# Splitting TensorE's two attention-times-V groups around the second pair of score matmuls, in a float32 transformer block on one core

## The chip, the cores and the metric

The kernel runs on one core of one Trainium2 chip. The metric is the device time of one execution in microseconds (us); 0.2% of it is 3.5 us. The profile adds one execution recorded instruction by instruction. The engines are PE (TensorE's matmuls), PEld (TensorE's weight loads), DVE (VectorE), ACT (ScalarE), POOL (GpSimd) and SP (SyncE, which issues DMAs).

## The reference

One transformer block with conditioning, for x of shape (4, 1024, 512), 16 heads of 32, in float32:

```
ada = silu(c) @ Wada.T + bada                      # shifts, scales and gates
h = modulate(rmsnorm(x, g1, D), scale_msa, shift_msa)
qkv = h @ Wqkv.T + bqkv
q = rmsnorm(q, gq, hd) * hd ** (-0.5);  k = rmsnorm(k, gk, hd)
attn = softmax(q @ k.T);  o = attn @ v
x = x + gate_msa * (o @ Wproj.T + bproj)
h = modulate(rmsnorm(x, g2, D), scale_mlp, shift_mlp)
x = x + gate_mlp * (gelu(h @ Wfc1.T + bfc1) @ Wfc2.T + bfc2)
```

## The kernel before, in words

Attention runs in 256 numbered steps L = 0 to 255, after 30 steps of start (L = -30 to -1); then comes the MLP. Each engine runs its own loop over L, written out by hand, and semaphores tie the loops together. A step covers four heads, 128 keys and 512 queries. Its parts:

- **Scores** `qk(L, p)`, p = 0 and 1 (line 558): two matmuls into the PSUM pair `scores[p]`. They wait until ACT has taken the exponentials of step L - 1 out of the same pair.
- **Exponentials** on ACT (line 784): two per step, into `probs[L % 3]`. The first of step L waits for `weigh(L - 3)` and for DVE's sum of step L - 3, since three `probs` buffers are there.
- **Weighing** `weigh(l)` (line 575): attention times V for step l, four matmuls with 32 columns of weights each, side by side in the array, into `pv`. A float32 matmul shows as two records, so one `weigh` is 8 records in the trace and 4 instructions in the program's order. All other matmuls named here use the full 128 x 128 array, apart from `row_sums` (lines 592 and 598), which also works in tiles of 32 columns. A run of such 32-column matmuls with nothing between them is called a **session** below.
- **Products** `fill(L, part)` (lines 645 and 658): the q, k and v projections of this and the next batch element. A table, `PLAN`, spreads each product of 12 matmuls over 1, 2 or 3 steps; half of a step's share is `part` 0 and half is `part` 1. All products accumulate in the one PSUM bank `gemm`, so the first matmul of a product waits until DVE has moved the last product out (`raw_out`, line 896, or `v_out`, line 906). FILL, the steps with products, ends at L = 207 (`PAIRED`). For L from 3 on there are 84 products: 53 start in an odd step and 31 in an even one. Until step 59 all of them start in odd steps.
- **Sums** on DVE (line 871): `probs` is added up, one addition of 128 x 2048 per step. In DVE's step L the order is: the last product's move-out, then `add(L - 1)`, then the pieces of the q and k norms.
- **Norm pieces**: `sum_squares` (lines 606, 610, 611), `turn` (transposes, line 622) on PE; logarithm, exponential and squares on ACT.

Through step 207, PE weighs in pairs: in each odd step, after all products of the step, it runs `weigh(L - 2)` and `weigh(L - 1)` as one session. From step 208 on it weighs once a step. `row_sums` (for L = 9, 17, 25, ..., always odd) stands between `qk(L, 0)` and `fill(L, 0)` up to L = `EARLY` = 80, and right ahead of the pair of weighings after that.

`TAIL` is 214. It places the loads and first splits of the MLP's inputs: POOL issues the loads of `heads_first` (line 1323) in its steps 216, 219, 222 and 225, and in step 216 it first waits for the last `part_lo`, which DVE makes in step 213. ACT splits them (line 1233) in steps 232 to 238.

Of the kernel before, what the change touches and what calls it, by code (L numbers as in the profile page):

```python
# [94 lines left out]
FILL = {step + i: (p, kind, b, g, x, i, steps) for p, (step, steps, b, kind, g, x) in enumerate(PLAN) for i in range(steps)}  # L95
# [9 lines left out]
def at_row(when):  # L105
    return {NT * (hh + 1) + when: hh for hh in range(NC * NG - 1)}


ROWS_AT, COMPACT_AT, INVERT_AT, INVERTED_AT, SPREAD_AT, OUT_AT = (at_row(x) for x in (ROWS, COMPACT, INVERT, INVERTED, SPREAD, OUT))
# [11 lines left out]
EARLY = 5 * STEPS  # L121
# [34 lines left out]
INV_AT, FIN_AT = ({step + after: n for step, n in SUM_AT.items()} for after in (1, 2))  # L156
LOW_AT = {step + (n >= HALVED): n for step, n in FIN_AT.items()}
# [4 lines left out]
def adds_until(l):  # L162

    hh, j = l // NT, l % NT
    return ADDS * min(hh, LEAN) + (ADDS - 1) * max(0, hh - LEAN) + (min(j, ADDS - 1) if hh >= LEAN else j)
# [6 lines left out]
    at = first + NT * (half + 1) + (-1 if kind == "k" else 3) if step >= 0 else step + 3  # L172
    STACK_LOAD.setdefault(max(step + 1, at), []).append(n)

TAIL = max(LOW_AT) + 1
PRODUCT_OF_UNIT = [p for p, x in enumerate(PLAN) if x[3] != "v"]
PRODUCT_OF_V = [p for p, x in enumerate(PLAN) if x[3] == "v"]
LOADED = 4
# [1 line left out]
PAIRED = max(FILL)  # L180
HEADS_LOAD, BIAS_LOAD, X_LOAD = {TAIL + 2 + 3 * t: t for t in range(CT)}, TAIL + 14, {TAIL + 17 + 3 * t: t for t in range(CT)}
HEADS_HIGH, HEADS_LOW, X_BIASED = ({TAIL + after + 2 * t: t for t in range(CT)} for after in (18, 19, 34))
MOD_LOAD, SCALE = 8, 14
# [171 lines left out]
def build_attention(nc, sem, small, dram, mem, psum, mlp):  # L355
# [181 lines left out]
    def tensor(pe):  # L537
# [3 lines left out]
        def qk(L, p):  # L541
            group, st = L // STEPS, L % STEPS
            half, j = st // NT, st % NT
            s = group % 2
            if p == 0:
                if st == 0 or st == NT // 2:
                    pe.wait_ge(k_in[s][st // (NT // 2)], 64 * (group // 2 + 1))
                if j == 0:
                    pe.wait_ge(q_in[half], 64 * (group + 1))
            if L > 0:  # L550

                pe.wait_ge(exp_done, 2 * (L - 1) + p + 1)
            elif p == 0:
                pe.wait_ge(h_moved, NT // 2)
                pe.wait_ge(h_moved_too, NT // 2)
            for i in range(2):
                h = 2 * p + i
                mm = nc.tensor.matmul(scores[p][:, i, :], k_stack[s][:, h, j * P:(j + 1) * P], q_stack[half][:, h, :],  # L558
                                      start=True, stop=True)
            mm.then_inc(qk_mm, 1)  # L560

        def weigh(l):
            b, g, j, hh = l // BSTEPS, l // STEPS % NG, l % NT, l // NT
            pe.wait_ge(exp_done, 2 * l + 2)
            if l == 0:

                last = max(p for p in range(FIRST_PRODUCTS) if p % 2 == 1)
                pe.wait_ge(v_moved if PLAN[last][3] == "v" else raw_done, NUMBER[last] + 1)
            if l % BSTEPS < NT:
                pe.wait_ge(v_moved, b * NT + j + 1)  # L570
            if j == 0 and hh >= NH:

                pe.wait_ge(o_done, hh - NH + 1)
            for h in range(HG):
                mm = nc.tensor.matmul(pv[hh % NH][h * DH:(h + 1) * DH, :], v[b % 2][:, j, (g * HG + h) * DH:(g * HG + h + 1) * DH],  # L575
                                      probs[l % RING][:, h, :], start=(j == 0), stop=(j == NT - 1))
            mm.then_inc(pv_mm, 1)

        def aux_free():

            if issued["squares"]:
                pe.wait_ge(ln_done, issued["squares"])
            if issued["turns"] > NT:
                pe.wait_ge(*moved(issued["turns"] - 1))
            if issued["rows"]:
                pe.wait_ge(rows_moved, issued["rows"])

        def row_sums(hh):
            pe.wait_ge(added, adds_until(NT * hh + NT - 1))
            aux_free()  # L590
            for h in range(HG):
                mm = nc.tensor.matmul(aux[h * DH:(h + 1) * DH, :], small["ones"][:], sums[:, h, :], start=True, stop=(hh < LEAN))  # L592
            if hh >= LEAN:

                l = NT * hh + NT - 1
                pe.wait_ge(exp_done, 2 * l + 2)
                for h in range(HG):
                    mm = nc.tensor.matmul(aux[h * DH:(h + 1) * DH, :], small["ones"][:], probs[l % RING][:, h, :], start=False, stop=True)
            mm.then_inc(rs_mm, 1)
            issued["rows"] += 1  # L600
# [33 lines left out]
        def unit_products(p, which, b, g, half, lo, hi):  # L634

            at = (0 if which == "q" else D) + g * P
            c = slice(half * CH, (half + 1) * CH)
            terms = [(w, h, k) for k in range(KT) for w, h in ((wq_hi, h_hi), (wq_hi, h_lo), (wq_lo, h_hi))]
            if lo == 0:
                bank_free(p)  # L640
                pe.wait_ge(lo_done, b * NT + (half + 1) * CT)
                pe.wait_ge(setup["low"], (1 if which == "k" else 2) + (3 if g > 0 else 0))
            for n in range(lo, hi):
                w, h, k = terms[n]
                mm = nc.tensor.matmul(bank_of_product(p)[:], w[:, k, at:at + P], h[:, k, c], start=(n == 0), stop=(n == len(terms) - 1))  # L645
            if hi == len(terms):
                mm.then_inc(unit_mm, 1)

        def v_products(p, b, t, lo, hi):
            c = slice(t * P, (t + 1) * P)  # L650
            terms = [(h, w, k) for k in range(KT) for h, w in ((h_hi, wq_hi), (h_hi, wq_lo), (h_lo, wq_hi))]
            if lo == 0:
                bank_free(p)
                pe.wait_ge(lo_done, max(CT, b * NT + t + 1))
                pe.wait_ge(setup["low"], 3)
            for n in range(lo, hi):
                h, w, k = terms[n]
                mm = nc.tensor.matmul(bank_of_product(p)[:], h[:, k, c], w[:, k, 2 * D:3 * D], start=(n == 0), stop=(n == len(terms) - 1))  # L658
            if hi == len(terms):
                mm.then_inc(v_mm, 1)  # L660

        def fill(L, part):
            if L not in FILL:
                return
            p, kind, b, g, x, i, steps = FILL[L]
            per = 3 * KT // steps
            lo = i * per + part * (per // 2)
            hi = lo + per // 2
            if kind == "v":
                v_products(p, b, x, lo, hi)  # L670
            else:
                unit_products(p, kind, b, g, x, lo, hi)

        setup["tensor_first"](pe)
        for L in range(START, AFTER):
            if L >= 0:
                qk(L, 0)
            if L in ROWS_AT and L <= EARLY:
                row_sums(ROWS_AT[L])
            fill(L, 0)  # L680
            if L >= 0:
                qk(L, 1)
            if L in ROWS_AT and L > PAIRED:
                row_sums(ROWS_AT[L])
            fill(L, 1)
            if L in SUM_AT:
                sum_squares(SUM_AT[L])
            if L in ROW_MM:
                setup["tensor_row"](pe, ROW_MM[L])
            if L in TURN_AT:  # L690
                turn(TURN_AT[L])
            if L == MOD_TURN:
                setup["tensor_turn"](pe)
            if L == NT:
                pe.wait_ge(ada_made, NA_LATER)
            if L in ROWS_AT and EARLY < L <= PAIRED:
                row_sums(ROWS_AT[L])
            if L > PAIRED:
                weigh(L - 1)
            elif L > 0 and L % 2 == 1:  # L700

                if L > 1:
                    weigh(L - 2)
                weigh(L - 1)
            if L == ADA_MM:
                for k in range(KT):
                    for i, r in enumerate(ada_rows):
                        if k == 0:
                            pe.wait_ge(ada_w_in[i], 16)
                        mm = nc.tensor.matmul(pv[1][r, :], silu[:, k, :], ada_w[i][:, k, :], start=(k == 0), stop=(k == KT - 1))  # L710
                mm.then_inc(ada_mm, 1)
# [143 lines left out]
    def vector(dve):  # L855
# [172 lines left out]
        mlp_last(lambda: invert(last), lambda: output(last))  # L1028

    return dict(sync=sync, tensor=tensor, scalar=scalar, gpsimd=gpsimd, vector=vector)  # L1030


# [821 lines left out]
```

## Time and profile before

| what | value |
|---|---|
| device time, three runs | median 1774.96 us (1774.0 to 1777.69) |
| the profiled execution | 1777.33 us |
| its span, first to last instruction | 1775.5 us |
| PE busy | 1716.7 us, 97% |
| PEld busy | 1151.9 us, 65% |
| DVE busy | 1054.5 us, 59% |
| ACT busy | 976.0 us, 55% |

The profiled execution lasts 1.8 us longer than its span and stands 2.4 us above the median. Busy is the time in which at least one instruction of the engine runs. Matmuls overlap: one of 512 columns is recorded as about 390 ns long while the next starts 230 ns after it, so a busy PE may still lose time between matmuls. What a place costs on PE is read from the distance between the starts of matmuls.

Attention's steps 0 to 59 lie from 63 to 317 us of the span, steps 60 to 207 from 317 to 830 us, steps 208 to 255 from 830 to 956 us, and the MLP after that.

### The profile page before, as it was taken

To read this page: it belongs to the slowest core of one execution; us is meant where nothing else is said; L and a number is where in the kernel's file an instruction comes from. 1 tells how busy PE (TensorE), PEld (TensorE's weight loads), DVE (VectorE), ACT (ScalarE), POOL (GpSimd) and SP (SyncE) were. 2 spreads that over 40 slices of the span, in tenths; PEclk is the share of its full clock that TensorE was granted. 3 is DMA by queue.
4 is the path that set the end of the run, shared out by engine and by line. 5 is a ranking of instruction groups with operands and counts; after the bars stand their busy time and mean duration, and the time that the engine had idled before them with its cause. 6 is when DMAs were issued, how large, how long until landed. Compare 5 with 4: busy or idle time off the path is not lost.

```text
span 1775.5 us, 23481 instructions
## 1 busy us (share of the span) xinstructions
PE 1716.7 (97%) x8436; PEld 1151.9 (65%) x8436; DVE 1054.5 (59%) x1269; ACT 976.0 (55%) x1272; POOL 393.9 (22%) x303
## 2 busy tenths in 40 slices
PE   7999999999999999999999999999999999999999
PEld 4555554555555555554334787888888888888887
DVE  5678887889998899888687444141332324141311
ACT  4577777798888888879897432222222222222221
POOL 2001110111111111000150233333332333333332
PEclk9999999999999999999999899999999999999999
DMA  7555554555565554655775202010020202010000
GB/s 279 139 137 144 131 142 127 132 138 149 138 162 131 138 147 129 158 141 145 175 159 209 65 18 61 23 54 24 14 69 6 65 18 65 18 53 24 14 22 24
DMA packets 122244, 176.94 MB, mean 100 GB/s; under 512 B 29568, under 2 KB 43904, under 8 KB 121136
## 3 DMA queue, kind: packets, MB, share of 16 engines
q1 hardware_dynamic: 119648, 163.75, 34.5%
q10 hardware_dynamic: 1712, 9.47, 1.4%
q0 software_dynamic: 800, 2.62, 0.6%
q8 instruction: 50, 0.82, 0.2%
q14 instruction: 34, 0.28, 0.1%
HBM read 124.87 MB, written 50.92 MB: 99 GB/s over the span
## 4 chain that ended last, share of the span: by engine, by line
PE 74%; DVE 12%; ACT 7%; issue 4%; DMA 2%; SPq 1%; POOL 0%; ACTq 0%; DVEq 0%
PE scores L1446 19%; PE pv L1463 10%; PE gemm L1463 10%; PE scores L558 8%; PE pv L575 7%; DVE sums L871 7%; PE gemm L645 6%; ACT probs L784 5%; PE pv L1418 4%; PE gemm L658 4%; PE aux L592 2%; DVE raw L896 1%; DMA parts_scratch<-parts 1%; DVE h_full L936 1%; PE aux L1433 1%
## 5 line engine op out<-in xcount | busy, mean ns | idle before, releaser
L784 ACT ACTIVATE probs<-scores,shift 128x1024 f32<-128x1024 f32 x512 | 549.9, 1115 | 141.9 <-PE scores L558 133.3
L871 DVE TENSOR_TENSOR sums<-sums,probs 128x2048 f32<-128x2048 f32 x186 | 440.0, 2366 | 26.4 <-ACT probs L784 23.6
L558 PE MATMUL scores<-q_stack,k_stack 128*128 128x512 f32 x1024 | 349.2, 425 | 5.5 <-ACT probs L784 4.3
L1446 PE MATMUL scores<-w_hi,act_parts 128*128 128x512 f32 x1016 | 315.0, 391 | 0.0
L558 PEld LDWEIGHTS scores<-q_stack,k_stack 128*128 128x128 f32 x1024 | 172.2, 188 | 191.8 <-issue 92.0
L1378 POOL TENSOR_TENSOR act_parts<-act_full,act_parts 128x512 fp32r<-128x512 f32 x127 | 170.4, 1342 | 477.2 <-ACT act_parts L1309 477.2
L575 PE MATMUL pv<-probs,v 128*32 128x512 f32 x2048 | 251.3, 599 | 2.3 <-DVE o_out L881 1.9
L1446 PEld LDWEIGHTS scores<-w_hi,act_parts 128*128 128x128 f32 x1016 | 189.2, 188 | 38.3
L1309 ACT ACTIVATE act_parts<-act_full 128x512 fp32r<-128x512 f32 x127 | 80.3, 632 | 219.7 <-PE scores L1446 218.8
L1446 PE MATMUL scores<-w_lo,act_parts 128*128 128x512 f32 x508 | 197.9, 389 | 0.0
L1522 DVE TENSOR_TENSOR y_next<-pv,p_bias 128x512 f32<-128x512 f32 x28 | 19.3, 691 | 298.5 <-PE pv L1418 298.5
L1463 PE MATMUL gemm<-z,w 128*128 128x512 f32 x768 | 187.1, 393 | 2.6 <-DVE z L1627 2.6
L1463 PE MATMUL pv<-z,w 128*128 128x512 f32 x768 | 185.7, 391 | 0.0
L1463 PEld LDWEIGHTS gemm<-z,w 128*128 128x128 f32 x768 | 145.7, 190 | 33.4 <-DVE z L1627 3.0
L1463 PEld LDWEIGHTS pv<-z,w 128*128 128x128 f32 x768 | 144.0, 188 | 29.9
L1295 ACT ACTIVATE act_full<-gemm,f_bias 128x512 f32<-128x512 f32 x64 | 44.2, 690 | 186.7 <-PE gemm L1463 181.4
L575 PEld LDWEIGHTS pv<-probs,v 128*32 128x32 f32 x2048 | 53.1, 109 | 124.6 <-issue 109.8
L645 PE MATMUL gemm<-h_hi,wq_hi 128*128 128x512 f32 x248 | 103.9, 419 | 22.4 <-DVE raw L896 12.0
L1295 ACT ACTIVATE act_full<-pv,f_bias 128x512 f32<-128x512 f32 x64 | 44.0, 688 | 147.4 <-PE pv L1463 146.0
L840 POOL TENSOR_TENSOR h_lo<-h_full,h_hi 128x512 fp32r<-128x512 f32 x26 | 73.2, 2817 | 217.0 <-ACT h_hi L765 217.0
L1446 PEld LDWEIGHTS scores<-w_lo,act_parts 128*128 128x128 f32 x508 | 95.4, 188 | 20.1
L845 POOL TENSOR_TENSOR x_inv<-x_sqc,minus_half 128x1 f32<-128x1 f32 x32 | 18.8, 589 | 390.5 <-DVE x_sqc L918 390.5
(195 smaller groups left out, 2059.6 us busy)
## 6 DMA issues: line engine op xcount, KB each, us to landing
k_stack<-parts_scratch SPq DMA_DIRECT2D x128, 256.0 KB, 5.0
q_stack<-parts_scratch SPq DMA_DIRECT2D x128, 256.0 KB, 5.1
parts_scratch<-parts SPq DMA_DIRECT2D x62, 512.0 KB, 3.1
inverse<-inverse_scratch SPq DMA_DIRECT2D x128, 64.0 KB, 2.0
heads_out<-o_out SPq DMA_DIRECT2D x32, 256.0 KB, 4.7
out<-result SPq DMA_DIRECT2D x30, 256.0 KB, 2.0
heads<-heads_out SPq DMA_DIRECT2D x28, 256.0 KB, 3.9
x_tile<-in_x SPq DMA_DIRECT2D x28, 256.0 KB, 2.8
```

Of the source, the lines that this page charges most:

```text
L558: mm = nc.tensor.matmul(scores[p][:, i, :], k_stack[s][:, h, j * P:(j + 1) * P], q_stack[half][:, h, :], start=True, stop=True)
L575: mm = nc.tensor.matmul(pv[hh % NH][h * DH:(h + 1) * DH, :], v[b % 2][:, j, (g * HG + h) * DH:(g * HG + h + 1) * DH], probs[l % RING][:, h ...
L645: mm = nc.tensor.matmul(bank_of_product(p)[:], w[:, k, at:at + P], h[:, k, c], start=(n == 0), stop=(n == len(terms) - 1))
L658: mm = nc.tensor.matmul(bank_of_product(p)[:], h[:, k, c], w[:, k, 2 * D:3 * D], start=(n == 0), stop=(n == len(terms) - 1))
L784: nc.scalar.activation(probs[L % RING][:, 2 * p:2 * p + 2, :], scores[p][:], ACT.Exp, bias=small["shift"][:]).then_inc(exp_done, 1)
L840: nc.gpsimd.tensor_tensor(h_lo[:, :, c], buffer_of_turn(n)[:], full(h_hi[:, :, c]), ALU.subtract).then_inc(lo_done, 1)
L871: nc.vector.tensor_tensor(sums[:], a[:], probs[l % RING][:], ALU.add).then_inc(added, 1)
L1295: nc.scalar.activation(act_full[m % 2][:], up[m % 2], ACT.Gelu_apprx_tanh, bias=f1_bias[:, m:m + 1]).then_inc(gelu_done, 1)
L1309: nc.scalar.activation(parts_of(c, m)[:, 0, :], act_full[m % 2][:], ACT.Copy).then_inc(act_hi, 1)
L1378: nc.gpsimd.tensor_tensor(parts_of(c, m)[:, 1, :], act_full[m % 2][:], full(parts_of(c, m)[:, 0, :]), ALU.subtract).then_inc(act_lo, 1)
L1446: mm = nc.tensor.matmul(acc[t], parts_of(c, m)[:, b, t * P:(t + 1) * P], w2[a][:, m, :], start=(m == 0 and i == 0), stop=(m == NM - 1 and ...
L1463: mm = nc.tensor.matmul(up[m % 2], w1[a][:, m, k, :], z[b][:, k, :], start=(k == 0 and i == 0), stop=(k == KT - 1 and i == 2))
```

## The change

In every odd step L > 1 that has products, PE's order becomes: `qk(L, 0)`, `weigh(L - 2)`, `qk(L, 1)`, `weigh(L - 1)`, both halves of the products, then the norm pieces. `row_sums` keeps its place up to L = 80; after that it stands behind `qk(L, 1)`, ahead of `weigh(L - 1)`. Even steps and all steps from 208 on are as before. `TAIL` becomes 212, the last entry of FIN_AT.

```
-TAIL = max(LOW_AT) + 1
+TAIL = max(FIN_AT)
...
         for L in range(START, AFTER):
+            weigh_first = L > 1 and L % 2 == 1 and L in FILL
             if L >= 0:
                 qk(L, 0)
             if L in ROWS_AT and L <= EARLY:
                 row_sums(ROWS_AT[L])
-            fill(L, 0)
+            if weigh_first:
+                weigh(L - 2)
+            else:
+                fill(L, 0)
             if L >= 0:
                 qk(L, 1)
-            if L in ROWS_AT and L > PAIRED:
+            if L in ROWS_AT and (L > PAIRED or weigh_first and L > EARLY):
                 row_sums(ROWS_AT[L])
+            if weigh_first:
+                weigh(L - 1)
+                fill(L, 0)
             fill(L, 1)
...
-            if L in ROWS_AT and EARLY < L <= PAIRED:
+            if L in ROWS_AT and EARLY < L <= PAIRED and not weigh_first:
                 row_sums(ROWS_AT[L])
             if L > PAIRED:
                 weigh(L - 1)
-            elif L > 0 and L % 2 == 1:
+            elif L > 0 and L % 2 == 1 and not weigh_first:
```

This is PE's order in step 57, where a v product starts (`gemm` is its bank, `pv<-probs` is a weighing, `aux<-sums` is `row_sums`). First before, from `qk(57, 0)` to the first scores of step 58:

```order
L558 MATMUL scores<-q_stack_69,k_stack_67 128x512 x2
L592 MATMUL aux<-sums,ones 32x512 x4
L658 MATMUL gemm<-wq_hi,h_hi 128x512
L658 MATMUL gemm<-wq_lo,h_hi 128x512
L658 MATMUL gemm<-wq_hi,h_lo 128x512
L558 MATMUL scores<-q_stack_69,k_stack_67 128x512 x2
L658 MATMUL gemm<-wq_hi,h_hi 128x512
L658 MATMUL gemm<-wq_lo,h_hi 128x512
L658 MATMUL gemm<-wq_hi,h_lo 128x512
L575 MATMUL pv<-probs_73,v_70 32x512 x4
L575 MATMUL pv<-probs_74,v_70 32x512 x4
L558 MATMUL scores<-q_stack_69,k_stack_67 128x512 x2
```

And after the change:

```order
L558 MATMUL scores<-q_stack_69,k_stack_67 128x512 x2
L592 MATMUL aux<-sums,ones 32x512 x4
L575 MATMUL pv<-probs_73,v_70 32x512 x4
L558 MATMUL scores<-q_stack_69,k_stack_67 128x512 x2
L575 MATMUL pv<-probs_74,v_70 32x512 x4
L658 MATMUL gemm<-wq_hi,h_hi 128x512
L658 MATMUL gemm<-wq_lo,h_hi 128x512
L658 MATMUL gemm<-wq_hi,h_lo 128x512
L658 MATMUL gemm<-wq_hi,h_hi 128x512
L658 MATMUL gemm<-wq_lo,h_hi 128x512
L658 MATMUL gemm<-wq_hi,h_lo 128x512
L558 MATMUL scores<-q_stack_69,k_stack_67 128x512 x2
```

The product's first matmul moved behind both weighings and the second pair of scores. The count of sessions is two in both.

The second place is the border of steps 157 and 158 on PE: a q product ends in step 157 and a v product starts in step 158. Before, from `qk(157, 1)` on:

```order
L558 MATMUL scores<-q_stack_69,k_stack_67 128x512 x2
L645 MATMUL gemm<-h_lo,wq_hi 128x512
L645 MATMUL gemm<-h_hi,wq_lo 128x512
L610 MATMUL aux<-squares_hi,head_ones 128x512
L611 MATMUL aux<-squares_lo,head_ones 128x512
L575 MATMUL pv<-probs_74,v_70 32x512 x4
L575 MATMUL pv<-probs_72,v_70 32x512 x4
L558 MATMUL scores<-q_stack_69,k_stack_67 128x512 x2
L658 MATMUL gemm<-wq_hi,h_hi 128x512
```

And after the change, from `qk(157, 0)` on:

```order
L558 MATMUL scores<-q_stack_69,k_stack_67 128x512 x2
L575 MATMUL pv<-probs_74,v_70 32x512 x4
L558 MATMUL scores<-q_stack_69,k_stack_67 128x512 x2
L575 MATMUL pv<-probs_72,v_70 32x512 x4
L645 MATMUL gemm<-h_hi,wq_lo 128x512
L645 MATMUL gemm<-h_hi,wq_hi 128x512
L645 MATMUL gemm<-h_lo,wq_hi 128x512
L645 MATMUL gemm<-h_hi,wq_lo 128x512
L610 MATMUL aux<-squares_hi,head_ones 128x512
L611 MATMUL aux<-squares_lo,head_ones 128x512
L558 MATMUL scores<-q_stack_69,k_stack_67 128x512 x2
L658 MATMUL gemm<-wq_hi,h_hi 128x512
```

Between the end of one product and the start of the next, the two weighings are gone, and one session became two.

## Rows read from the trace of the kernel before

**Rows 1.** The page, part 1: busy time, share, instructions

```profile
PE 1716.7 (97%) x8436; PEld 1151.9 (65%) x8436; DVE 1054.5 (59%) x1269; ACT 976.0 (55%) x1272; POOL 393.9 (22%) x303
```

**Rows 2.** Busy us (x instructions) by stretch, then clock, DMA share, GB/s

```profile
core 0: us, PE busy (x) PEld busy (x) DVE busy (x) ACT busy (x) POOL busy (x), PEclk, DMA share, GB/s
63.00:317.00 254.00, 239.40 (x1220) 138.23 (x1224) 202.97 (x224) 185.24 (x225) 23.42 (x19) 0.99 0.51 136
317.00:830.00 513.00, 499.15 (x2726) 277.87 (x2719) 448.98 (x421) 439.76 (x546) 60.46 (x29) 1.00 0.55 141
```

**Rows 3.** Timeline, end of step 171: start us, length us, engine, line, tiles

```profile
706.86 0.40 PE L645 MATMUL gemm<-h_hi,wq_hi 128*128 128x512 f32 x1
...
707.18 1.92 PE L575 MATMUL pv<-probs,v 128*32 128x512 f32 x16
...
709.04 0.73 PE L558 MATMUL scores<-q_stack,k_stack 128*128 128x512 f32 x2
...
709.61 0.39 PE L645 MATMUL gemm<-h_lo,wq_hi 128*128 128x512 f32 x1
```

**Rows 4.** Timeline, step 210, where a session holds one weighing

```profile
838.61 0.40 PE L611 MATMUL aux<-squares_lo,head_ones 128*128 128x512 f32 x1
...
838.93 1.06 PE L575 MATMUL pv<-probs,v 128*32 128x512 f32 x8
...
839.93 1.54 PE L558 MATMUL scores<-q_stack,k_stack 128*128 128x512 f32 x4
```

**Rows 5.** Timeline of PE, step 25: row sums, then a product

```profile
172.16 1.07 PE L592 MATMUL aux<-sums,ones 128*32 128x512 f32 x8 [0.35 <-issue]
173.15 0.50 PE L645 MATMUL gemm<-h_hi,wq_hi 128*128 128x512 f32 x1
```

**Rows 6.** Waits of PEld, 63 to 317 us: total, times, longest

```profile
PEld gemm L645 <- DVE raw L896: 15.6, 13, 3.0
PEld gemm L645 <- DVE v L906: 4.3, 5, 1.6
...
PEld gemm L658 <- DVE raw L896: 3.6, 4, 1.8
...
PEld gemm L658 <- DVE v L906: 2.4, 3, 0.8
```

**Rows 7.** Waits of PEld, 317 to 830 us

```profile
PEld scores L558 <- ACT probs L784: 28.9, 67, 0.8
PEld gemm L658 <- DVE raw L896: 13.7, 15, 2.2
...
PEld gemm L645 <- DVE raw L896: 9.3, 14, 1.5
PEld gemm L645 <- DVE v L906: 6.2, 13, 0.8
```

**Rows 8.** Timeline, steps 170 and 171: a product ends, the next starts

```profile
703.67 0.62 PE L558 MATMUL scores<-q_stack,k_stack 128*128 128x512 f32 x2
...
704.13 0.40 PE L645 MATMUL gemm<-h_lo,wq_hi 128*128 128x512 f32 x1
...
704.36 0.39 PE L645 MATMUL gemm<-h_hi,wq_lo 128*128 128x512 f32 x1
...
704.79 0.75 DVE L896 TENSOR_SCALAR raw<-gemm,qk_bias 128x512 f32<-128x512 f32 x1 [0.26 <-PE gemm L645]
...
705.60 0.19 PEld L645 LDWEIGHTS gemm<-h_hi,wq_hi 128*128 128x128 f32 x1 [0.38 <-DVE raw L896]
```

**Rows 9.** Timeline, step 158: a product starts in an even step

```profile
661.07 0.73 PE L558 MATMUL scores<-q_stack,k_stack 128*128 128x512 f32 x2
661.25 0.74 DVE L896 TENSOR_SCALAR raw<-gemm,qk_bias 128x512 f32<-128x512 f32 x1
...
662.04 0.19 PEld L658 LDWEIGHTS gemm<-wq_hi,h_hi 128*128 128x128 f32 x1 [0.68 <-DVE raw L896]
662.04 0.50 PE L658 MATMUL gemm<-wq_hi,h_hi 128*128 128x512 f32 x1 [0.24 <-DVE raw L896]
662.15 0.19 PEld L658 LDWEIGHTS gemm<-wq_lo,h_hi 128*128 128x128 f32 x1
662.38 0.40 PE L658 MATMUL gemm<-wq_lo,h_hi 128*128 128x512 f32 x1
```

**Rows 10.** Waits of ACT, 317 to 830 us

```profile
ACT probs L784 <- PE scores L558: 64.4, 78, 1.9
```

**Rows 11.** Timeline of POOL: the first load of the MLP's heads

```profile
852.70 0.95 POOL L1323 DMA_DIRECT2D y<-heads_out  x1 [139.06 <-issue]
```

## The prediction

> **What bounds the kernel now.** The change sits in steps 3 to 207, so I looked at that stretch only. The page comes first [rows 1]: PE is busy for 97% of the span, with DVE and ACT far behind. By stretch the picture is closer [rows 2]: from 317 to 830 us PE is busy 499 of 513 us (97%), DVE 449 (88%) and ACT 440 (86%); from 63 to 317 us they are at 94%, 80% and 73%. So PE is first, and the other two follow closely in the later stretch.
>
> Busy time hides what PE loses, so I read starts. In an undisturbed stream full-array matmuls start 0.23 us apart: the two score matmuls at 703.67 take 0.46 us until the next product matmul, and that one 0.23 until the next [rows 8]. Two things break the stream. One is a session of 32-column matmuls. The other is the start of a product, whose first weight load waits for DVE to move the last product out [rows 6, 7]. The sum is made of these two.
>
> The Trainium skill ("Perfetto Trace Analysis", Identifying the Most-Contended Engine) says that matmul busy time is a bad measure and that the busy share of weight loads is a good one. By the weight loads [rows 2] TensorE works 278 of 513 us, 54%, which would leave DVE as the most contended engine and would make extra time on PE free. The starts speak against it here: nearly all of PE's time is taken by matmuls at their closest spacing or by a session. I take the starts, and keep the page's reading as a rival, worked out from rows below.
>
> **Term A: more sessions.** A session of two weighings spreads the last full matmul ahead of it and the first behind it 709.04 - 706.86 = 2.18 us apart [rows 3]. With one weighing it is 839.93 - 838.61 = 1.32 us [rows 4]. So a weighing costs 0.86, and a session by itself 1.32 - 0.86 = 0.46 where an undisturbed distance is 0.23: 0.23 lost. The two score matmuls behind a session then take 709.61 - 709.04 = 0.57 until the next start [rows 3], not 0.46 [rows 8]: 0.11 more. A session more costs 0.34 us. The change also puts a product behind a session; the nearest row is a product behind row sums, whose first matmul starts 0.99 after the session's start [rows 5], as scores do in step 210 (1.00) [rows 4], so the price is the same.
>
> How many more: odd steps 3 to 207 are 103. Where row sums stand at L up to 80 (9 to 73, nine steps) there were two sessions and there are two; in later steps with row sums they already shared the session of the weighings and still share one. So 103 - 9 = 94 more, 94 x 0.34 = **+32 us**. It lies on the path wherever PE doesn't wait anyway. "TensorEngine Tiling (Array Packing)", Key Properties, of the Trainium skill says that changing the tiling mode drains TensorE. It names no price; it speaks against this change, and without such a drain A would be nothing and the sum below lower by 32.
>
> **Term B: product starts in odd steps.** The first product matmul now comes behind two sessions and four score matmuls, about 2.5 us later (the wait for DVE counts from the end of the last product, and that end, in an even step, isn't moved). What is lost at such a start is PEld's idle time less 0.17: in step 158 the idle is 0.68 [rows 9], while the product starts 0.97 after the scores where 0.57 is undisturbed [rows 3], and its second matmul 0.34 after the first and not 0.23, together 0.51. Until 317 us the waits sum to 25.9 us in 25 starts, less 25 x 0.17 gives 21.6 [rows 6]. All but steps 0 and 2 start in odd steps. Step 1 isn't changed (0.6), and the longest (3.0) keeps a few tenths: 20 go. From 317 us on it is 29.2 in 42 starts, less 42 x 0.17 gives 22 [rows 7]. Of these, even starts have about 9: seven like step 158 at 0.51, two long ones (the longest row, 2.2) at 2.0, the rest 0.1 each. The odd ones' 13 go. B = **-33 us**. Bounds: all of the 43.6 read as odd and gone, -43; or, if DVE is late by more than the 2.5 us in some, -28.
>
> **Term C: product starts in even steps.** Here the change takes cover away. Before, a product that ended in an odd step had the session of two weighings behind it: DVE could start up to 2.5 us late and the next product still lost only 0.1 to 0.5. Now only two score matmuls stand between. The smallest distance from a product's last matmul to the next product's first, with DVE free, is 705.60 - 704.36 = 1.24 us [rows 8]; the undisturbed one is 3 x 0.23 = 0.69. That loses 0.55, and 0.11 for the second matmul: 0.65 per start. Of the 31 even starts, 12 have a `sum_squares` ahead of them at the end of the odd step (as step 158), which gives 0.46 of cover: 0.1 to 0.3 each. 19 have none: 19 x 0.65 = 12.4. With 12 x 0.25 = 3 and 3.5 for the two long ones, where DVE is late by more than that, even starts lose 19 in place of 9. C = **+10 us**. Bounds: +4 (the later end of the product finds the stall of the two long ones and of the seven gone, and DVE always free) to +25 (DVE late by half an addition more at each).
>
> **Term D: waits for exponentials.** `qk(L, 1)` of an odd step now stands behind `weigh(L - 2)`, 0.6 us later, and no longer catches ACT at work. PEld's idle time for scores, released by ACT, is 28.9 us in 67 [rows 7], but most of it is the ordinary wait behind a session that ends with ACT's signal as the last one. I take -2, between 0 and -5. `qk(L, 0)` waits as before, since the even step ahead of it is the same.
>
> **Term E: TAIL.** POOL's loads wait for a signal of DVE's step 213 in either kernel, and POOL has nothing else queued: the first goes out at 852.70 after 139 us of nothing [rows 11]. Moving it from POOL's step 216 to 214 moves no issue in time. ACT's four splits come two steps earlier, the same number in the same stage. 0, between -1 and +1. What covers it is the rest of attention, to 956 us; if that were gone, a load moved by two steps would cost what it is late, at most its few us once.
>
> **Sum.** 32 - 33 + 10 - 2 = +7 us on the profiled execution's 1777.33: 1784. That execution stood 2.4 above the median 1774.96, so against the median it is **1782 us**.
>
> **Rivals.**
> - *DVE becomes the bound (slower by more).* In DVE's program the addition of step L stands behind the move-out in step L + 1, and that now waits until the end of the odd step. DVE is at 88% [rows 2]. If each of the 31 even starts holds an addition up by 0.5 us and it isn't made good, C grows by 15: 1797. For it: the high share. Against: the pair gets longer by 0.34, which gives DVE room. From 2 or 3 tenths of DVE's time per pair on it decides. Chance 0.15.
> - *TensorE isn't the bound (the other side).* ACT waits for scores 64.4 us in 78 times from 317 to 830 us [rows 10], all while PE is in its double session. With the scores of p = 1 between the two weighings, ACT gets them spread out, DVE's additions come earlier, and its lateness at starts of both kinds goes. Then sessions are paid from time in which PE waited: B -40, C +2, D -5, with A 32: -11, so 1764. It needs DVE on time at three quarters of the starts. For it: ACT's long waits. Against: a free DVE still loses 0.65 per even start, and ACT isn't what PE waits for most. Chance 0.25 for anything faster than -3.5, the likeliest of it near 1768. The page's reading of TensorE ends here as well, since it would make A free.
> - *The terms cancel (no change).* A and C at the low end, B at the middle: 30 - 33 + 6 - 2 = +1, 1776. Chance 0.2.
> - *The forecast,* +3.5 to +15: chance 0.4.
>
> **How the numbers follow.** Faster 0.25; within 0.2% (3.5 us, about what a measurement of this kernel can tell from no change) 0.2; slower 0.4 + 0.15 = 0.55. The range leaves out the far tenth on each side: from 1767, most of the way into the fast rival, to 1796, up to the DVE rival. The forecast's own range is 1778 to 1790.
>
> **What the changed kernel's profile would show.** A: in odd steps two rows of 8 weighing records with a score pair between, each pair behind one with 0.73 length; PE's record count as before. B: the stretch up to step 59 shorter than 254 us by about 12 (20 saved, 22 sessions x 0.34 = 7.5 paid), with waits of `gemm` for DVE nearly gone there. C: after that the stretch to step 207 longer than 513 us by about 19, waits of `gemm` loads at even starts at 0.7 to 1 us each. E: first head load still right behind the last `part_lo`. The prediction is wrong if the second stretch doesn't grow: then either sessions overlap with waits or DVE was late for a reason that the new order removes. It is wrong the other way if DVE's additions wait for move-outs and ACT for additions.

## The result: 1800 us, slower by 1.35%

| | before | after |
|---|---|---|
| device time, four runs each | 1776.33 us (1774.0 to 1779.04) | 1800.28 us (1798.96 to 1801.02) |
| ratio | | 1.0135 (95% interval 1.0123 to 1.0147) |
| span of the profiled execution | 1775.5 us | 1797.1 us |
| steps 0 to 59 | 255.4 us | 258.7 us |
| steps 60 to 207 | 512.7 us | 532.8 us |
| steps 208 to 255 | 123.7 us | 122.5 us |

A stretch of steps goes here from the first score matmul of its first step to the first one behind its last step; the last row ends at the first score matmul of step 255, since none comes behind it. In the kernel before, step 60 starts at 318.3 us and step 208 at 831.0, 1.3 and 1.0 us later than the 317 and 830 that the forecast went by; this moves none of its terms. The kernel is slower by 24 us where +7 was forecast. The later stretch grew by 20.1 us (forecast 19.5). The early one, which was to shrink by 12, grew by 3.3. The miss is there.

The page of the kernel after, part 1 (as [rows 1]) and part 4, the chain that ended last, by engine:

```profile
PE 1740.0 (97%) x8436; PEld 1138.0 (63%) x8436; DVE 1054.4 (59%) x1269; ACT 977.7 (54%) x1272; POOL 385.4 (21%) x303
PE 82%; DVE 10%; ACT 5%; issue 2%; DMA 1%; SPq 0%; POOL 0%; DVEq 0%; ACTq 0%
```

PE's busy time rose by 23 us and its share stayed, because the profile counts as busy what is lost between matmuls. The number of PE instructions is the same (8436). Busy time by stretch, before and then after; the columns are those of [rows 2], the stretches those of the table:

```profile
62.90:318.30 255.40, 240.77 (x1229) 138.49 (x1229) 204.27 (x225) 186.07 (x227) 23.88 (x20) 0.99 0.52 136
318.30:831.00 512.70, 498.85 (x2722) 277.84 (x2718) 448.79 (x421) 439.99 (x545) 60.00 (x29) 1.00 0.55 140
```

```profile
61.70:320.40 258.70, 244.13 (x1229) 134.59 (x1230) 205.97 (x226) 183.37 (x225) 19.95 (x19) 0.99 0.51 135
320.40:853.20 532.80, 518.92 (x2720) 268.23 (x2719) 448.00 (x422) 444.90 (x546) 55.87 (x29) 1.00 0.53 135
853.20:975.70 122.50, 117.17 (x656) 38.94 (x654) 92.67 (x54) 107.78 (x112) 28.81 (x19) 1.00 0.62 150
```

DVE and ACT work nearly as long as before in each stretch (in the later one DVE 449 and then 448 us, ACT 440 and 445), and the granted clock is the same. So the time is in the order, not in slower instructions. To find it I went through the starts of PE's matmuls and took from each distance the undisturbed one of [rows 3, 4, 8]; what is left is a stall, named by what stands ahead of it and behind it. A sum of many stalls depends on the undisturbed distance that is taken off, and is good to about 1 us:

| us of stall on PE | before | after | forecast |
|---|---|---|---|
| **steps 1 to 59**, sessions | 37 | 59 | +22, +7.5 us |
| product starts, both their matmuls | 19.0 | 4.5 | -20 |
| row sums, waiting for the sum | 1.4 | 9.2 | 0 |
| sum of squares at the end of an even step | 0 | 1.7 | 0 |
| all stalls of the stretch | 30.0 | 26.9 | -20 |
| **steps 60 to 206**, sessions | 75 | 146 | +72, +24.5 us |
| product starts in odd steps, both matmuls | 13.2 | 0.3 | -13 |
| product starts in even steps, both matmuls | 9.3 | 15.5 | +10 |
| scores of odd steps behind products, waiting for ACT | 1.7 | 6.4 | 0 |
| second matmul of the score pairs in odd steps | 5.6 | 3.6 | -2 |
| all stalls of the stretch | 32.7 | 29.1 | -5 |

The later part of the table ends where step 207 starts, so it has 71 new sessions and not 72. Sessions at 0.34 us and stalls add up to the change over the same steps: 22 x 0.34 - 3.1 = +4.4 us (measured +3.3), and 71 x 0.34 - 3.6 = +20.5 us (measured +19.7).

**Where the early 20 us went.** PE's waits from 61.7 to 320.4 us, which answer to [rows 6], total, times, longest:

```profile
PEld aux L592 <- DVE sums L878: 6.5, 3, 2.4
...
PEld gemm L645 <- DVE raw L903: 5.1, 4, 1.9
...
PEld gemm L645 <- DVE v L913: 3.4, 3, 1.7
...
PEld gemm L658 <- DVE raw L903: 2.9, 2, 2.0
...
PEld gemm L658 <- DVE v L913: 1.6, 2, 0.8
```

The waits at product starts did shrink, from 25.9 us in 25 starts to 13.0 in 11, and of those 13.0 0.84 each is the ordinary pause of a load behind a session (a row with it, 674.87, is shown below), so 3.8 us are lost, near the 4.5 of the table. The first row is new: `row_sums` (L592) waits for DVE's addition. It stands in PE's queue ahead of `weigh(L - 2)`, which has no reason to wait. DVE's own waits in the same stretch show why its addition is late:

```profile
DVE sums L878 <- ACT probs L791: 18.5, 11, 4.2
DVE h_full L943 <- PE aux L622: 8.5, 4, 2.6
```

Before, `h_full` waited 0.5 us in 2 times. `h_full` moves the four transposes of `turn` out of PSUM, and in DVE's order the next addition stands behind it. In the new order `turn` comes last in PE's step. Step 35 and the start of step 36 in the timeline, first before, then after (DVE and PE rows):

```profile
213.63 2.28 DVE L871 TENSOR_TENSOR sums<-sums,probs 128x2048 f32<-128x2048 f32 x1
...
215.47 0.60 PE L622 MATMUL aux<-ident,xt 128*128 128x128 f32 x4
...
216.11 1.37 DVE L936 TENSOR_SCALAR h_full<-aux,scale,mod 128x128 f32<-128x128 f32 x4 [0.20 <-PE aux L622]
...
217.40 2.28 DVE L871 TENSOR_TENSOR sums<-sums,probs 128x2048 f32<-128x2048 f32 x1
```

```profile
212.97 2.28 DVE L878 TENSOR_TENSOR sums<-sums,probs 128x2048 f32<-128x2048 f32 x1
...
217.22 0.60 PE L622 MATMUL aux<-ident,xt 128*128 128x128 f32 x4
...
217.85 1.36 DVE L943 TENSOR_SCALAR h_full<-aux,scale,mod 128x128 f32<-128x128 f32 x4 [2.60 <-PE aux L622]
219.14 2.28 DVE L878 TENSOR_TENSOR sums<-sums,probs 128x2048 f32<-128x2048 f32 x1
```

The addition ahead of it ends 0.66 us earlier than before, the next one starts 1.74 us later. The 2.4 us between the two are the wait in brackets, 2.60 where it was 0.20: DVE stands still, because both sessions of the step, which came behind `turn`, now stand ahead of it. In step 41, after one more such `turn` in step 39, PE waits 1.94 us for an addition at the row sums (new kernel):

```profile
236.41 2.28 DVE L878 TENSOR_TENSOR sums<-sums,probs 128x2048 f32<-128x2048 f32 x1
...
238.74 1.06 PE L592 MATMUL aux<-sums,ones 128*32 128x512 f32 x8 [1.94 <-DVE sums L878]
```

**Where the later 20 us come from.** A session's end and an even start of the new kernel, steps 157 and 158, which answer to [rows 9]:

```profile
674.87 0.19 PEld L645 LDWEIGHTS gemm<-h_hi,wq_lo 128*128 128x128 f32 x1 [0.84 <-issue]
...
675.67 0.40 PE L645 MATMUL gemm<-h_hi,wq_lo 128*128 128x512 f32 x1
...
676.11 0.75 DVE L903 TENSOR_SCALAR raw<-gemm,qk_bias 128x512 f32<-128x512 f32 x1
...
676.38 0.62 PE L558 MATMUL scores<-q_stack,k_stack 128*128 128x512 f32 x2
...
676.91 0.50 PE L658 MATMUL gemm<-wq_hi,h_hi 128*128 128x512 f32 x1
```

The product in step 158 starts 676.91 - 676.38 = 0.53 us behind the scores, so it loses 0.07 us, where it took 0.97 before. The even starts that have no `sum_squares` ahead of them now lose time instead, and all even starts sum to 15.5 us. The later stretch is thus made of term A's 24 us and of stalls that nearly cancel.

### The profile page after: what moved, and what is told of

Read it like the earlier page. It is cut to its first block, busy times and chain, and to the rows that moved or that the text cites. A ratio compares the mean times of both kernels' runs of the same rounds, so it can differ in the third digit from the quotient of the medians.

```text
span 1797.1 us, 23481 instructions
## 1 busy us (share of the span) xinstructions
PE 1740.0 (97%) x8436; PEld 1138.0 (63%) x8436; DVE 1054.4 (59%) x1269; ACT 977.7 (54%) x1272; POOL 385.4 (21%) x303
## 4 chain that ended last, share of the span: by engine, by line
PE 82%; DVE 10%; ACT 5%; issue 2%; DMA 1%; SPq 0%; POOL 0%; DVEq 0%; ACTq 0%
PE scores L1453 19%; PE pv L575 10%; PE scores L558 10%; PE pv L1470 10%; PE gemm L1470 10%; PE gemm L645 8%; DVE sums L878 5%; PE gemm L658 4%; PE pv L1425 4%; ACT probs L791 3%; PE aux L592 2%; PE aux L606 1%; PE aux L1440 1%; DVE h_full L943 1%; DVE v L913 1%
## 5 line engine op out<-in xcount | busy, mean ns | idle before, releaser
L878 DVE TENSOR_TENSOR sums<-sums,probs 128x2048 f32<-128x2048 f32 x186 | 437.5, 2352 | 25.1 <-ACT probs L791 21.9
L558 PE MATMUL scores<-q_stack,k_stack 128*128 128x512 f32 x1024 | 348.1, 424 | 10.2 <-ACT probs L791 9.2
L575 PE MATMUL pv<-probs,v 128*32 128x512 f32 x2048 | 273.2, 605 | 0.5 <-ACT probs L791 0.4
L847 POOL TENSOR_TENSOR h_lo<-h_full,h_hi 128x512 fp32r<-128x512 f32 x26 | 65.3, 2510 | 226.9 <-ACT h_hi L772 226.9
L575 PEld LDWEIGHTS pv<-probs,v 128*32 128x32 f32 x2048 | 43.6, 108 | 102.0 <-issue 73.1
```

What stands on the lines that cost most here:

```text
L878: nc.vector.tensor_tensor(sums[:], a[:], probs[l % RING][:], ALU.add).then_inc(added, 1)
```

## The experiments

Each kernel is the kernel before with one edit to PE's order, and each was timed in five rounds against the kernel before on the same chip. `TAIL` is as before in all but the tenth. The condition `weigh_first` of the change says in which odd steps the new order holds.

**1 and 2. Early steps alone, later steps alone.**

```
-            weigh_first = L > 1 and L % 2 == 1 and L in FILL
+            weigh_first = 1 < L < 60 and L % 2 == 1                  # first kernel
+            weigh_first = L >= 60 and L % 2 == 1 and L in FILL       # second kernel
```

> The new order in odd steps 3 to 59 alone; TAIL and all steps from 60 on as before. In the changed kernel steps 0 to 60 took 258.7 us (61.7 to 320.4) against 255.4 before, where I had forecast 12 less. If that miss is a thing of this stretch by itself (theory: DVE becomes late there and stays late), this kernel reads 3 to 5 us above before, and steps 0 to 60 last 258 to 260 us. Rival: the early gain is there, and is lost because the later steps' order reaches back through buffers; then this kernel is 8 to 12 us faster than before.

Measured: 1780.04 against 1775.99 us, ratio 1.0024 (1.0014 to 1.0035): +4.0 us.

> The new order in odd steps 61 to 207 alone. Terms A, C and the later part of B are what acts here: 72 sessions x 0.34 = +24.5, odd starts -13, even starts +10, waits for exponentials -2: +19.5 us over before, 1796. In the changed kernel steps 60 to 208 took 532.8 us against 512.7, which is +20. Rival: the loss needs the lateness that DVE brings along from the early steps; then +10 or less.

Measured: 1794.16 against 1775.99 us, ratio 1.0102 (1.0086 to 1.0117): +18.2 us. The two add to +22.2 us of the +24. The later part is as forecast; the early one costs time where it was to save 12.

**3. Transposes ahead of the products.** The first kernel, with `turn` right behind `weigh(L - 1)` in its odd steps:

```
             if weigh_first:
                 weigh(L - 1)
+                if L in TURN_AT:
+                    turn(TURN_AT[L])
                 fill(L, 0)
...
-            if L in TURN_AT:
+            if L in TURN_AT and not weigh_first:
                 turn(TURN_AT[L])
```

> As s1_only, and in odd steps with a turn (four transposes) those stand ahead of the step's products, behind weigh(L - 1), so that they end about 1.4 us sooner. Theory: the early gain is lost since DVE's h_out, which is queued ahead of add(L), waits for transposes that now come last in the odd step (8.5 us of such waits in the changed kernel against 0.5 before, in four places). Then those waits fall to 2 to 4 us, DVE is late by less at row sums and at the next starts, and the time is 4 to 8 us below s1_only. Rival (row sums are what waits, whatever DVE does; or DVE is simply full): within 2 us of s1_only.

Measured: 1775.08 against 1775.99 us, ratio 0.9997 (0.9988 to 1.0006), which is 5.0 us less than the first kernel. DVE's and PE's waits of it, 62.6 to 316.1 us:

```profile
DVE h_full L945 <- PE aux L622: 2.7, 4, 1.2
```

```profile
PEld aux L622 <- DVE xt L932: 5.5, 4, 2.5
...
PEld aux L592 <- DVE sums L880: 3.9, 3, 1.9
```

DVE's wait fell from 8.5 to 2.7 us. The row of L622 is the price: at its new place `turn` is early for its own input in four steps. The late transposes are a cause, but not the only reason why the row sums wait: their row is still 3.9 us, where it is 6.5 in the first kernel (shown in experiment 4). What else makes those additions late for PE was not separated.

**4. Row sums behind `qk(L, 1)`.** The first kernel, with early row sums where the change has the late ones:

```
-            if L in ROWS_AT and L <= EARLY:
+            if L in ROWS_AT and L <= EARLY and not weigh_first:
                 row_sums(ROWS_AT[L])
...
-            if L in ROWS_AT and (L > PAIRED or weigh_first and L > EARLY):
+            if L in ROWS_AT and (L > PAIRED or weigh_first):
```

> As s1_only, with the row sums of these steps behind qk(L, 1) and ahead of weigh(L - 1), where the later ones are. Rival theory: what was gained at starts is lost because row_sums stands right behind qk(L, 0) and waits for DVE's addition (9 us in seven steps in the changed kernel, 1.4 before) while weigh(L - 2) could run; then the time is 6 to 9 us below s1_only. Theory (DVE itself is late through the transposes): the wait only moves on to the product's start or the next additions, and the time is 0 to 3 us below s1_only.

Measured: 1772.75 against 1775.99 us, ratio 0.9984 (0.9975 to 0.9993), 7.3 us less than the first kernel. PE's waits in the first kernel, 62.5 to 321.2 us:

```profile
PEld aux L592 <- DVE sums L878: 6.5, 3, 2.5
...
PEld gemm L645 <- DVE raw L903: 6.0, 5, 1.9
```

DVE's and PE's waits in this one, 62.5 to 314 us:

```profile
DVE h_full L943 <- PE aux L622: 8.8, 4, 2.6
```

```profile
PEld aux L592 <- DVE sums L878: 1.9, 3, 0.8
...
PEld gemm L645 <- DVE raw L903: 8.8, 6, 2.4
```

My theory, that the place of the row sums is a symptom worth 0 to 3 us, fell, and the rival was right. `h_full` waits as long as in the full change, so DVE is no earlier; but the weighing ahead of the row sums now fills part of the time. A part moved on to the product starts (6.0 to 8.8 us). The number of sessions is 59 in both kernels, since the row sums only change from the session of `weigh(L - 2)` to that of `weigh(L - 1)`, so all of the 7.3 us are waits.

**5. Both at once.** Edits 3 and 4 in one kernel.

> s1_turn_first and s1_rows_later together, steps 3 to 59 alone. Alone they gave -5.0 and -7.3 us against s1_only. If late transposes and early row sums are two causes side by side, -10 to -12: 1768 to 1770. If they are one (either takes away the same lateness of DVE), -7 to -8: 1772 to 1773. My forecast of the stretch had been -12.5 against before, which would be 1763.5.

Measured: 1769.56 against 1775.99 us, ratio 0.9964 (0.9951 to 0.9978), 10.5 us less than the first kernel. 5.0 + 7.3 = 12.3: two causes side by side with an overlap of 2. Its steps 0 to 59 take 247.5 us where the kernel before takes 255.4 and the change 258.7. So these two edits get 8 of the forecast 12 us. In its trace product starts still lose 3.8 us and `turn` loses 2.1 waiting for its own input.

**6. One session of two weighings.** The change, with both weighings ahead of `qk(L, 1)`, and from step 81 on the row sums between them:

```
             if weigh_first:
                 weigh(L - 2)
+                if L in ROWS_AT and L > EARLY:
+                    row_sums(ROWS_AT[L])
+                weigh(L - 1)
             else:
                 fill(L, 0)
...
             if weigh_first:
-                weigh(L - 1)
                 fill(L, 0)
```

> The changed kernel's order, but both weighings in one session ahead of qk(L, 1) in all odd steps 3 to 207: qk(L, 0), weigh(L - 2), weigh(L - 1), qk(L, 1), products (row sums after step 80 between the weighings; TAIL as before). It leaves the late products, the late transposes and the short cover of even starts as they are and takes 103 sessions away. Term A says 103 x 0.34 = 35 us less than the changed kernel: 1765, 11 below before. Rival (TensorE's sessions are paid from waiting time, and what costs is the products' place): 1795 or more.

Measured: 1792.74 against 1775.99 us, ratio 1.0094 (1.0079 to 1.0109): only 7.5 us less than the full change. Neither theory holds as written. The sessions went (103 fewer, -35 us by term A), but stalls grew: from 26.9 to 30.2 us in steps 1 to 59, and from 29.1 to 50.9 in steps 60 to 206, of them 19.1 in place of 6.4 at the scores of odd steps behind products. ACT's and PE's waits in the later stretch, first of the change (320 to 853 us), then of this kernel (315 to 847 us), which also answer to [rows 7, 10]:

```profile
ACT probs L791 <- PE scores L558: 53.3, 83, 1.8
```

```profile
PEld scores L558 <- ACT probs L791: 42.2, 58, 2.0
```

```profile
ACT probs L793 <- PE scores L558: 81.9, 98, 2.6
```

```profile
PEld scores L558 <- ACT probs L793: 52.4, 65, 2.0
...
PEld aux L592 <- DVE sums L880: 10.9, 13, 1.5
```

With the double session ahead of `qk(L, 1)` ACT waits for its scores 82 us in place of 53, so it is later with the exponentials, and PE waits for those; its row sums wait for the additions, which are late with them. The second session costs 0.34 us and hands ACT its second pair one weighing sooner. Most of what it costs comes back there: 7.5 us of 35 are left.

**7 to 9. Later steps by their kind.** The 74 later odd steps are 24 in which a product starts, 32 in which one ends and 18 in its middle. Steps 73 (an end) and 65 (a middle) have early row sums and so two sessions in either order, which leaves 31 and 17 new sessions; the expectations counted one step too few for the ends and one too many for the middles. The new order in one kind each:

```
+            weigh_first = L >= 60 and L % 2 == 1 and L in FILL and FILL[L][5] == 0                    # starts
+            weigh_first = L >= 60 and L % 2 == 1 and L in FILL and FILL[L][5] == FILL[L][6] - 1       # ends
+            weigh_first = L >= 60 and L % 2 == 1 and L in FILL and 0 < FILL[L][5] < FILL[L][6] - 1    # middles
```

> The new order from step 60 on only in the 24 odd steps in which a product starts. Even starts keep their double session as cover, so term C falls away: 24 x 0.34 = +8, odd starts -13, exponentials -1: -6 us against before, 1770. s2_only had +18.2. Rival (what costs from step 60 on is the sessions and what they do to ACT and DVE, not the even starts): +18.2 x 24 / 72 = +6, 1782.

Measured: 1772.78 against 1775.99 us, ratio 0.9983 (0.9974 to 0.9992): -3.2 us, about half of the -6 expected. In its trace the 13.2 us at odd product starts are gone, but the scores of odd steps behind products lose the same 6.4 us for ACT as in the whole change. In the kernels of experiments 8 and 9 they stay under 2 us, so term D's miss comes from the start steps.

> The new order from step 60 on only in the 19 odd steps in which a product neither starts nor ends. Nothing of terms B and C is in it; 18 sessions more (step 65 has early row sums) at 0.34 = +6 us, 1782, if a session is paid in full. Rival (a session between the two score pairs feeds ACT more evenly and is half paid by waits that it takes away, which one_session's small gain hints at): +3 or less.

Measured: 1780.49 against 1776.29 us, ratio 1.0022 (1.0012 to 1.0031): +4.2 us, between the two: 0.25 us for each of the 17 new sessions. At 0.34 us these sessions would cost 5.8 us. In its trace stalls shrink by some 2.5 us from step 60 on, 1.7 of it at odd product starts (13.2 to 11.5), whose steps weren't changed. What is left, 3.3 us, is near the 3 us by which steps 60 to 207 grew (512.7 to 515.8): a session costs no less here, but stalls elsewhere pay a part of it.

> The new order from step 60 on only in the 31 odd steps in which a product ends, so that the next starts in the even step behind. 30 sessions more = +10 us and term C = +10: 1796. Against s2_only (+18.2), s2_starts (-3.2) and s2_mid (+6) additivity asks for +15 to +16. Rival (C is nothing, since DVE was late at those starts anyway): +10, 1786.

Measured: 1800.37 against 1776.29 us, ratio 1.0133 (1.0113 to 1.0154): +24.1 us, as slow as the whole change, with a third of its new sessions. PE's waits from 318 to 856 us:

```profile
PEld gemm L645 <- DVE raw L903: 16.2, 21, 1.9
...
PEld gemm L658 <- DVE raw L903: 15.3, 16, 3.3
...
PEld gemm L645 <- DVE v L913: 12.1, 16, 0.8
```

Its sessions went from 75 to 105 (+10.2 us) and its stalls from 32.7 to 47.6 us (+14.9); together +25.1, and steps 60 to 207 last 537.9 us, 25.2 more. Stalls at even starts rose from 9.3 to 17.3 us, and those at product starts in odd steps from 13.2 to about 19, though nothing was moved in those: DVE is late there too. Alone the three kinds sum to -3.2 + 4.2 + 24.1 = +25.1, together they are +18.2. So the new order in start steps is worth 18.2 - 24.1 - 4.2 = -10 us once the end steps have it, and -3 without: the stall that it takes away at odd starts is about 19 us in the one case and 13.2 in the other.

**10. TAIL alone.**

```
-TAIL = max(LOW_AT) + 1
+TAIL = max(FIN_AT)
```

> TAIL = 212 alone, nothing else changed: 0, within 1.5 us of before, since POOL's loads wait for DVE's step 213 in either. Rival: ACT's four splits meet other work in steps 230 to 236, +-2 us.

Measured: 1776.53 against 1776.29 us, ratio 0.9999 (0.9989 to 1.0008): nothing.

**11. New order where a product starts, one session.** In odd steps with `FILL[L][5] == 0` (29 early, 24 later) both weighings and row sums between them stand ahead of `qk(L, 1)`, and `turn` ahead of the products; all else is as before. From step 60 on every `turn` lies in an even step, so that part acts in the early steps alone.

> All that the theory asks for: only in the 53 odd steps in which a product starts, with both weighings in one session ahead of qk(L, 1), row sums between them, transposes ahead of the products. No session more than before (in 7 steps with early row sums one less, -2), even starts keep their cover, odd starts lose their stalls. Early stretch -20 at most, of which 12 to 18 if DVE keeps up, later -13 and -2: 1776 - 30 = 1746, between 1742 and 1756. Rival (DVE and ACT are so full that they take over): not below 1765.

Measured: 1767.3 against 1775.99 us, ratio 0.9952 (0.9938 to 0.9966): -8.7 us. Steps 0 to 59 take 245.0 us, 10.4 less than before, and steps 60 to 207 take 512.8, as long as before. The -30 us expected were far off, and the rival held. Later, odd starts lose nothing any more, but the scores of odd steps behind products lose some 19 us waiting for ACT, as in experiment 6. Early, 245.0 us is 2.5 less than with the split sessions of experiment 5; experiment 12 has the same early order and takes 246.7, so the lead of one session is 1 to 2.5 us, where 29 sessions less would have given 10.

**12. The parts that pay.** As 11 through step 59; from 60 on the split order in start steps.

```
+            weigh_first = L > 1 and L % 2 == 1 and L in FILL and FILL[L][5] == 0
+            together = weigh_first and L < 60
```

> In the 53 odd steps in which a product starts: up to step 59 both weighings in one session ahead of qk(L, 1), with the row sums between them (in best1 steps 1 to 60 lasted 241.2 us, 10.4 less than before); from step 60 on the changed kernel's split order (s2_starts: steps 60 to 207 at 505.2, in best1 508.4); transposes ahead of the products. -10.4 and -3.2: 1762 to 1764. Rival (the two stretches don't add up): 1767, as best1.

Measured: 1763.12 us (1762.28 to 1767.1) against 1776.29, ratio 0.993 (0.9914 to 0.9946): -13.2 us, faster than both kernels. Its stretches, with the columns of [rows 2]:

```profile
62.40:309.10 246.70, 235.02 (x1229) 138.12 (x1230) 204.93 (x225) 181.83 (x225) 18.96 (x19) 1.00 0.53 140
309.10:819.10 510.00, 501.19 (x2719) 275.31 (x2717) 449.30 (x421) 441.58 (x547) 54.87 (x29) 1.00 0.55 142
```

8.7 us come from the first stretch, 2.7 from the second and 2.1 from steps 208 to 255 (123.7 to 121.6), where nothing was changed. That last stretch lies between 121.4 and 124.7 us in the traces of all fourteen kernels (before, after and twelve experiments), which have the same order on PE there, so the 2.1 us can't be put down to this edit.

## Why the prediction was right in direction and wrong in size

The direction was right, the size (+24 us for +7) wasn't, and 1800.28 lies above the range.

- **Term B, early: the step that failed.** "20 go" of the 21.6 us until 317 us. By the distances between starts there were 19.0 us, and 14.5 of them went (19.0 to 4.5), but 8 came back at the row sums and 2 at the sum of squares of even steps, 2 more came in small pieces elsewhere, and all stalls together fell by 3. B took DVE's move-out as the only wait, and as one that is counted from the product's end alone. It left out that what was moved ahead of the products pushes everything behind them in PE's step: `turn` came 2.4 us later against DVE's addition (step 35), and DVE waits for it with an addition queued behind. Experiments 3 to 5 show both halves, 5.0 and 7.3 us, 10.5 together, and with them the early stretch comes to 247.5 us; the forecast was about 243. Of the 7.8 us at the row sums the transposes explain only a part (experiment 3); what else makes those additions late stays open. This is the rival "DVE becomes the bound" in kind, with its condition (additions that wait) met in the early stretch and through another instruction than the one I named.
- **Term A** was right in count and in price where the change is read as a whole: sessions at 0.34 us and the stalls account for both stretches within 1.1 us. Experiment 8 has a net of 0.25 us for a session, since stalls elsewhere shrink. What was wrong is that A stands by itself: experiment 6 takes the sessions away and gets 7.5 us of 35 back, because the split also brings ACT's scores forward. The rival "TensorE isn't the bound" said that sessions would be paid from PE's waits. That is true in part, but it needed DVE on time, and DVE was later.
- **Term B, later:** -13 forecast, -12.9 measured. **Term C:** +10 forecast, +6.2 in the change. Done alone, the end steps cost far more (experiment 9), which C couldn't see: it priced even starts with DVE free, and DVE isn't.
- **Term D** had the wrong sign: -2 forecast. The second matmuls of odd steps' score pairs lose 2.0 less, but the first pair behind a product loses 4.7 more, of which I wrote that it "waits as before, since the even step ahead of it is the same". The step is the same; what stands ahead of it isn't, and ACT comes into it later. Experiment 7 puts it on the start steps. C and D erred by 4 and 5 us against each other, and the later stretch came out within 0.6 us partly for that reason.
- **Term E:** 0, measured 0.2 in experiment 10.
- **The trace's busy shares.** I had set the Trainium skill's reading ("Perfetto Trace Analysis", Identifying the Most-Contended Engine: judge TensorE by its weight loads) against the starts of matmuls. In steps 60 to 207 the loads' share fell from 277.84/512.70 = 54% to 268.23/532.80 = 50% while the time grew by 20 us. By its direction the trace agrees with it, since the same work took longer. By its level the trace doesn't: 54% would leave room for new sessions, and 71 of them at 0.34 us were paid with only 3.6 us of stalls to set against them. On a change of tiling mode the Trainium skill ("TensorEngine Tiling (Array Packing)", Key Properties) says that it drains TensorE. The trace agrees in so far as each session costs time at its ends, 0.34 us; that this time is a drain, no row shows.

Two things stay open: why steps 208 to 255 differ by up to 3 us between kernels that don't differ there, and what besides the transposes makes the additions late at the row sums.

## What to carry to other kernels

Where something is moved ahead in an in-order queue, list what it pushes back, and for each of those the engine that waits and what that engine has queued behind the wait: here four small transposes, up to 2.4 us later, held up an addition, and putting them first gave 5.0 of the 15 us back by which the early stretch missed its forecast. Move work ahead only in the steps where it hides a wait (13 us faster), not in all of them (24 us slower). And a cost that is read between two matmuls of one engine isn't all to be had by taking it away, when its place also sets when the next engine can start.

## What the hardware showed that I had not expected

- A session of 32-column matmuls between full-array ones costs 0.34 us at its ends, read from the starts. But 103 more of them, in a kernel whose PE is at 97%, made 7.5 us (1800.28 against 1792.74) and not 35, because the same split hands ACT its scores sooner.
- DVE at 88% busy in a stretch is already late at the places that count. Its busy time there stayed within 1 us (448.8 before, 448.0 after, 449.7 in experiment 9), while PE's stalls in the stretch lay between 29.1 and 47.6 us by nothing but the order of PE's instructions.
